# Retrieval products of a two-layer decoder: float32 against three float32r products of split parts

## The chip, the cores and the metric

The kernel runs on one core of one Trainium2 chip. The metric is the device time of one execution in microseconds (us). TensorE is called PE in the rows (its weight loads PEld), VectorE is DVE, ScalarE is ACT, GpSimd is POOL, and SyncE, which issues most of the transfers, is SP.

## The reference

Two decoder layers run over 16 sequences of 128 rows with 256 channels. The change concerns the last sublayer, which this part of the reference describes (its selection of weights is told in words):

```
# x: [16, 128, 256];  gate_w, up_w: [256, 1024];  down_w: [1024, 256]
# down_embed, up_embed: [512, 256]
q        = x @ W_q                        # two halves of 64, scored against two sets of 64 keys
weights  = softmax over the best 8 pairs of keys, spread over the 512 experts
found    = silu(x @ down_embed.T) * weights                       # [.., 512]
out      = (silu(x @ gate_w) * (x @ up_w)) @ down_w + found @ up_embed
x        = layernorm(x + out)
```

All of it is float32. The layers before it are two attentions and a mixture of experts (first layer), and two attentions (second layer).

## The kernel before

The program is a row of stages, each a block in which every engine has its own ordered list of instructions and engines wait on each other by semaphores.

**The second layer** (`second_layer_attentions`, from line 1539) walks through numbered slots. A batch takes a window of 12 slots, and each operation has an offset (the constants before line 1610); each engine goes through the slots and does what falls due. `batch_at(s, offset)` tells which batch is due. SP moves the split parts of queries and keys into stacks by many 64 KB transfers (helper lines 360 to 374), loads rows and context, and in one slot, `SPLIT_KEYS + 3` (line 1669), issues the five loads of the retrieval's weights: gate_w, up_w and down_w of 1 MB each, up_embed and down_embed of 0.5 MB each. POOL splits float32 rows into bf16 parts (helper lines 336 to 342, and lines 2029 and 2033), gathers rows (line 2018) and takes roots (line 2023). ACT does the exponentials (line 1885) and most copies.

**The retrieval** (`retrieve_and_gate`, from line 2214) takes the 16 batches in four turns g of four batches (WIDE is 512 columns), and each turn in eight slabs u of 128 of the 1024 inner channels. The order of PE is written out (before line 2355):

- `gate_and_up(g, u)` (line 2315): two float32 products of 512 columns into the gate bank and two into the up bank. Both banks are double, so it waits until `multiply` is done with slab s-2.
- `find(g, m)` (line 2335), at even u: two products of 512 columns, the rows of one batch against the turned down_embed.
- `down(g, u)` (line 2326), one slab late: four products of 256 columns, the hidden slab against down_w, added into two banks over the whole turn.
- at odd u `turn_weighed` (line 2342, four transposes of the weighed matches), `turn_rows` of the next turn (lines 2301 and 2302, three transposes), `route` (line 2306), and `add_weighed` (line 2349): four products of 256 columns against up_embed into the same banks as `down`.

ACT does Silu of the gate bank (line 2391) and of what was found (2398), the copies out of the transposes' banks (2378, 2403, 2383) and the exponentials (2407), which need another activation table than Silu. DVE multiplies gate and up (`multiply`, line 2520) at the start of every slab; at even u it then picks maxima (`best`), runs `select_weights` and `weigh` (line 2511); at odd u `select_pairs`. At u = 0 it also adds up the rows of the turn before (`add_rows`, 2525), at u = 1 it takes their moments (`spread`, helper lines 464 to 468) and at u = 3 it ends them (`finish`, 2537). POOL has only the 16 roots (line 2442), and three iotas.

Of the kernel before, what the change touches and what calls it, by code (L numbers as in the profile page):

```python
# [8 lines left out]
BF16 = mybir.dt.bfloat16  # L9
I32 = mybir.dt.int32  # L10
# [4 lines left out]
P = 128  # L15
# [1522 lines left out]

def second_layer_attentions(nc, d, t, ps):

    ctx = ExitStack()
    with ctx:
# [27 lines left out]
        ones_row = sb("ones_row_bf", [2, YG * D], BF16)  # L1570

# [8 lines left out]
        ones_made, rows_set = sem("ones_made"), sem("rows_set")  # L1580
        var_m_made, rstd_m_made, var_l_made, rstd_l_made = sem("var_m_made"), sem("rstd_m_made"), sem("var_l_made"), sem("rstd_l_made")
# [28 lines left out]
        STORE_ROWS, TURN_X5, COPY_X5, MAKE_QUERIES, COPY_QUERIES, STORE_QUERIES = 71, 72, 72, 73, 73, 74  # L1610
        query_lane = slots.lane(OWN_SCORES, CROSS_SCORES, SELF1.banks, CROSS1.banks)
# [5 lines left out]
        def _(sp):  # L1617
# [30 lines left out]

            for b in range(2):
                load_rows(b)  # L1650
# [5 lines left out]
            for s in SLOTS:  # L1656
# [10 lines left out]
                if s == SPLIT_KEYS + 3:  # L1667
                    for source, dst in RETRIEVAL_LOADS:
                        sp.dma_start(t[dst][:, :, :], d[source].rearrange("(n p) f -> p n f", p=P)).then_inc(t["retrieval_loaded"], 16)
# [207 lines left out]
        def _(act):  # L1877
# [91 lines left out]

            def copy_queries(b):  # L1970
                if b >= 2:
                    act.wait_ge(queries_stored[b % 2], 16 * (b // 2))
                act.wait_ge(queries_made, b + 1)
                act.activation(queries[b % 2][:, :], small_bank[:, 0:P], ACT.Copy).then_inc(queries_copied, 1)

            for s in SLOTS:
# [31 lines left out]
                if (b := slots.batch_at(s, LAY_X3)) is not None:  # L2008
                    lay_x3(b)

        @block.gpsimd
        def _(pool):
# [33 lines left out]

            gather(0)
            gather(1)
            pool.memset(ones_row[:, :], 1.0).then_inc(ones_made, 1)
            for s in SLOTS:  # L2050
# [16 lines left out]
                if (b := slots.batch_at(s, SPLIT_QUERIES)) is not None:  # L2067
                    split_queries(b)

# [144 lines left out]
def retrieve_and_gate(nc, d, t, ps, out):  # L2214

    ctx = ExitStack()
    with ctx:
# [9 lines left out]
        x5_t = [sb(f"x5_t_{u}", [P, KT + 1, WIDE]) for u in range(2)]  # L2227
# [14 lines left out]
        hidden_t = [sb(f"hidden_t_{u}", [P, WIDE]) for u in range(3)]  # L2242
        found = [sb(f"found_{u}", [P, NEMB]) for u in range(2)]
        weighed = [sb(f"weighed_{u}", [P, NEMB]) for u in range(2)]
        weighed_t = [sb(f"weighed_t_{u}", [P, NEMB // P, P]) for u in range(2)]
# [8 lines left out]
        iotas_made, embed_turned, embed_copied = sem("iotas_made"), sem("embed_turned"), sem("embed_copied")  # L2254
# [9 lines left out]
        loaded, LOADED = t["retrieval_loaded"], t["retrieval_loads"]  # L2264
# [19 lines left out]
        def _(pe):  # L2284
# [19 lines left out]
            def route(g, m):  # L2304
                pe.wait_ge(rows_copied, TOGETHER * g + m + 1)
                pe.matmul(found_bank[:, 3 * P:4 * P], x5_t[g % 2][:, KT, m * P:(m + 1) * P], t["keys"][:, :], start=True, stop=True).then_inc(routed, 1)  # L2306

            def gate_and_up(g, u):
                s = SLABS * g + u
                if s >= 2:  # L2310
                    pe.wait_ge(gated_made, s - 1)
                    pe.wait_ge(hidden_made, s - 1)
                for bank, weights, made in ((gate_bank[s % 2], "gate_w", gate_made), (up_bank[s % 2], "up_w", up_made)):
                    for j in range(KT):
                        mm = pe.matmul(bank[:, :], t[weights][:, j, u * P:(u + 1) * P], x5_t[g % 2][:, j, :], start=(j == 0), stop=(j == KT - 1))  # L2315
                    mm.then_inc(made, 1)

            def down(g, u):
                s = SLABS * g + u
                pe.wait_ge(hidden_made, s + 1)  # L2320
                if u == 0 and g > 0:
                    pe.wait_ge(sum_made, TOGETHER * g)
                if s == 0:
                    pe.wait_ge(embed_copied, KT)
                for m in range(TOGETHER):
                    mm = pe.matmul(acc_bank[m // 2][:, m % 2 * D:(m % 2 + 1) * D], hidden_t[s % 3][:, m * P:(m + 1) * P], t["down_w"][:, u, :],  # L2326
                                   start=(u == 0 and m % 2 == 0), stop=(u == SLABS - 1), skip_group_check=True)
                mm.then_inc(down_made, 1)

            def find(g, m):  # L2330
                b = TOGETHER * g + m
                pe.wait_ge(embed_copied, KT)
                pe.wait_ge(route_copied, routes_before(g, m))
                for j in range(KT):
                    mm = pe.matmul(found_bank[:, :], x5_t[g % 2][:, j, m * P:(m + 1) * P], t["down_embed_t"][:, j, :], start=(j == 0), stop=(j == KT - 1))  # L2335
                mm.then_inc(found_made, 1)

            def turn_weighed(g, m):
                b = TOGETHER * g + m
                pe.wait_ge(weighed_made, b + 1)  # L2340
                for n in range(NEMB // P):
# [3 lines left out]
            def add_weighed(g, m):  # L2345
                b = TOGETHER * g + m
                pe.wait_ge(weighed_copied, b + 1)
# [300 lines left out]
```

## Time and profile before

| | |
|---|---|
| time, median of 3 runs | 1685.72 us (1685.56 to 1687.22) |
| the profiled execution: span from first to last instruction | 1684.2 us |
| PE busy | 1400.9 us (83%) |
| DVE busy | 982.0 us (58%) |
| ACT busy | 609.2 us (36%) |
| POOL busy | 419.8 us (25%) |
| chain that ended last: share by PE | 13% |

The page gives no time of the profiled execution beside its span, so the span is its own time; the median of the runs lies 1.5 us above it. Busy shares are averages over all stages; the last stage, the retrieval, lasts from 1419 us to the end.

### The profile page before, as it was taken

How to read it: one execution, taken by the hardware profiler on the slowest of the kernel's cores; microseconds unless marked ns; L12 is line 12 of the kernel's file. 1: busy time of each engine (PE TensorE's matmuls, PEld its weight loads, DVE VectorE, ACT ScalarE, POOL GpSimd, SP SyncE). 2: the span in 40 equal slices, each digit the busy share in tenths (PEclk: the TensorE clock that was granted, in tenths of full speed). 3: DMA queues.
4: the chain of work that ended last, by engine and by line, in shares of the span. 5: the costliest groups of instructions: out<-in, count | busy, mean ns of one | idle time of the engine just before them, and what ended most of it. 6: DMA issues, size and time to landing. Idle time of an engine off the chain costs nothing. (4 is left out here: it accounts for less than half of the span.)

```text
span 1684.2 us, 29387 instructions
## 1 busy us (share of the span) xinstructions
PE 1400.9 (83%) x9221; PEld 874.6 (52%) x9331; DVE 982.0 (58%) x2623; ACT 609.2 (36%) x1389; POOL 419.8 (25%) x588
## 2 busy tenths in 40 slices
PE   2478999999999954899999946588888875999997
PEld 1245565665665522466566524455555543566654
DVE  5467788787777624222222224577788651676775
ACT  0123444544544421223222223255566542232321
POOL 2242342342341101011111023455555310000000
PEclk9679999999999976999999976799999996999999
DMA  3233443333432106611111123745454311100000
GB/s 91 59 66 60 70 72 52 72 70 55 72 67 37 24 27 226 225 32 38 32 32 33 28 56 109 159 105 114 107 116 111 85 34 50 38 1 13 13 1 26
DMA packets 165337, 112.77 MB, mean 67 GB/s; under 512 B 32690, under 2 KB 155826, under 8 KB 165056
## 3 DMA queue, kind: packets, MB, share of 16 engines
q1 hardware_dynamic: 150272, 99.04, 26.1%
q0 software_dynamic: 3408, 9.31, 2.3%
q10 hardware_dynamic: 11504, 2.53, 0.8%
q8 instruction: 78, 1.28, 0.4%
q14 instruction: 75, 0.61, 0.2%
HBM read 46.48 MB, written 12.45 MB: 35 GB/s over the span
## 5 line engine op out<-in xcount | busy, mean ns | idle before, releaser
L892 ACT ACTIVATE first_probs<-pair 128x512 f32<-128x512 f32 x320 | 189.0, 598 | 231.0 <-PE pair L408 217.4
L449 DVE TENSOR_REDUCE first_negmax_x<-bank 128x2 f32<-128x512 f32 x256 | 177.1, 692 | 59.7 <-PE bank L393 39.8
L393 PE MATMUL bank<-kept_stack_cross 96*128 96x256 bf16 x768 | 151.9, 280 | 11.8 <-DMA kept_stack_cross<-second_parts_x_q 7.5
L1885 ACT ACTIVATE second_probs<-pair 128x512 f32<-128x512 f32 x192 | 113.7, 598 | 130.8 <-PE pair L408 111.6
L408 PE MATMUL pair<-kept_stack_cross 98*128 98x256 bf16 x768 | 148.1, 275 | 3.0 <-ACT first_probs L892 1.0
L1439 PE MATMUL pair<-kept_w,experts_hidden_t 128*128 x312 | 140.5, 593 | 0.0
L449 DVE TENSOR_REDUCE second_negmax_x<-bank 128x2 f32<-128x512 f32 x128 | 88.6, 692 | 59.6 <-PE bank L393 50.5
L393 PEld LDWEIGHTS bank<-kept_stack_cross 96*128 96x128 bf16 x768 | 74.4, 102 | 73.0 <-issue 21.6
L1480 ACT ACTIVATE experts_hidden_t<-bank,kept_b 128x128 f32<-128x128 f32 x156 | 44.6, 368 | 186.4 <-PE bank L1414 186.4
L1394 POOL DMA_INDIRECT experts_expert_rows<-x_mid,kept_row_of x39 | 37.2, 953 | 275.6 <-PE bank L1406 249.1
L386 PE MATMUL bank<-kept_mask_q,kept_ident 128*128 128x512 bf16 x221 | 86.4, 391 | 20.4 <-DVE first_negmax_x L449 11.8
L1439 PEld LDWEIGHTS pair<-kept_w,experts_hidden_t 128*128 128x128 f32 x312 | 59.5, 191 | 74.8 <-issue 74.8
L401 PE MATMUL pair<-kept_mask_t,kept_ident 128*128 128x512 bf16 x249 | 94.7, 380 | 1.8 <-ACT first_probs L892 1.8
L408 PEld LDWEIGHTS pair<-kept_stack_cross 98*128 98x128 bf16 x768 | 74.2, 99 | 41.0 <-issue 2.2
L1517 DVE COPY experts_hidden<-pair 128x512 f32<-128x512 f32 x39 | 27.0, 692 | 107.7 <-PE pair L1439 107.7
L1430 PE MATMUL bank<-kept_w,experts_expert_rows_t 128*128 x156 | 76.8, 617 | 6.3 <-DMA kept_w<-in_L_ffn_W 2.8
L1448 PE MATMUL pair<-kept_w,experts_hidden_t 128*128 x312 | 73.9, 380 | 1.4 <-ACT experts_hidden_t L1488 1.4
L2442 POOL TENSOR_TENSOR retrieve_stats<-retrieve_stats,kept_minus_half 128x1 f32<-128x1 f32 x16 | 8.9, 558 | 251.4 <-DVE retrieve_stats L468 251.4
L438 PE MATMUL pair<-first_probs,kept_v_cross 128*32 128x256 f32 x1024 | 68.5, 385 | 2.8 <-ACT first_probs L892 2.8
L1511 DVE COPY experts_hidden<-bank 128x512 f32<-128x512 f32 x39 | 27.0, 692 | 71.6 <-PE bank L1430 71.6
L1488 ACT ACTIVATE experts_hidden_t<-bank,kept_b 128x128 f32<-128x128 f32 x156 | 44.7, 368 | 50.3 <-PE bank L1422 50.3
L2315 PE MATMUL pair<-retrieve_x_t,kept_gate_w 128*128 128x512 f32 x128 | 61.9, 607 | 0.0
(430 smaller groups left out, 2947.2 us busy)
## 6 DMA issues: line engine op xcount, KB each, us to landing
kept_stack_self<-first_parts_a SPq DMA_DIRECT2D x128, 64.0 KB
kept_w<-in_L_ffn_W SPq DMA_DIRECT2D x16, 512.0 KB, 9.1
kept_w<-in_L_ffn_W SPq DMA_DIRECT2D x8, 1024.0 KB, 9.5
kept_stack_self<-second_parts_a SPq DMA_DIRECT2D x128, 64.0 KB
kept_stack_cross<-first_parts_x_k SPq DMA_DIRECT2D x96, 64.0 KB
kept_stack_cross<-first_parts_x_q SPq DMA_DIRECT2D x96, 64.0 KB
kept_stack_cross<-second_parts_x_k SPq DMA_DIRECT2D x96, 64.0 KB
kept_stack_cross<-second_parts_x_q SPq DMA_DIRECT2D x96, 64.0 KB
```

The costliest lines, as they stand in the source:

```text
L386: pe.matmul(bank[:, :], ident16, mask, start=True, stop=False, skip_group_check=True)
L393: mm = pe.matmul(out, q, k, start=mask is None, stop=True, skip_group_check=True)
L401: pe.matmul(bank[:, :], ident16, mask, start=True, stop=False, skip_group_check=True)
L408: mm = pe.matmul(out, k, q, start=mask is None, stop=True, skip_group_check=True)
L438: mm = pe.matmul(out[j * 32:(j + 1) * 32, at * D:(at + 1) * D], values[:, 2 * k + at, a, j, :], probs[j][:, k * D:(k + 1) * D], start=(a = ...
L449: return dve.tensor_reduce(negmax[:, 2 * n:2 * n + 2], bank[:, :].rearrange("p (m t) -> p m t", t=D), AX.X, ALU.max, negate=True)
L892: act.activation(probs[i % RING][:, :], key_bank[i % 2][:, :], ACT.Exp, scale=att.scale).then_inc(probs_made, 1)
L1430: mm = pe.matmul(layer1_bank[:, :], rows_t[n % 2][:, k, :], t["w1"][:, bass.ds(expert, 1), k, :].rearrange("p a f -> p (a f)"), start=(k = ...
L1439: mm = pe.matmul(layer2_bank[:, :], hidden1_t[n % 2][:, k, :], t["w2"][:, bass.ds(expert, 1), k, :].rearrange("p a f -> p (a f)"), start=( ...
L1448: mm = pe.matmul(layer3_bank[:, 0:D], hidden2_t[n % 2][:, k, :], t["w3"][:, bass.ds(expert, 1), k, :].rearrange("p a f -> p (a f)"), start ...
L1885: act.activation(probs[i % RING][:, :], key_bank[i % 2][:, :], ACT.Exp, scale=att.scale).then_inc(probs_made, 1)
L2315: mm = pe.matmul(bank[:, :], t[weights][:, j, u * P:(u + 1) * P], x5_t[g % 2][:, j, :], start=(j == 0), stop=(j == KT - 1))
```

## The change

Every large float32 product of the retrieval becomes three products of the type float32r. Each operand is kept as a high part (the value written as float32r by ACT) and a low part (the value minus the high part, by POOL, or by DVE for down_embed). `in_parts` multiplies low by high, high by low and high by high. Transposes and `route` stay float32.

```diff
+            def in_parts(to, still, moving, start, stop):
+                (still_high, still_low), (moving_high, moving_low) = still, moving
+                pe.matmul(to, still_low, moving_high, start=start, stop=False, skip_group_check=True)
+                pe.matmul(to, still_high, moving_low, start=False, stop=False, skip_group_check=True)
+                return pe.matmul(to, still_high, moving_high, start=False, stop=stop, skip_group_check=True)
 ...
             def gate_and_up(g, u):
+                if u == 0:
+                    pe.wait_ge(rows_split, TOGETHER * (g + 1))
 ...
-                        mm = pe.matmul(bank[:, :], t[weights][:, j, u * P:(u + 1) * P], x5_t[g % 2][:, j, :], start=(j == 0), stop=(j == KT - 1))
+                        mm = in_parts(bank[:, :], [w[:, j, u * P:(u + 1) * P] for w in t[weights]], [x[:, j, :] for x in x5_t[g % 2]], j == 0, j == KT - 1)
 ...
             def down(g, u):
-                pe.wait_ge(hidden_made, s + 1)
+                pe.wait_ge(hidden_split, s + 1)
```

`down`, `find` and `add_weighed` are changed likewise. `add_weighed` moves from the end of the odd slab to the next even slab, behind `down(g, u - 1)`; that of the turn's last batch stands ahead of the turn's last `down`:

```diff
                 gate_and_up(g, u)
                 if u % 2 == 0:
                     if u == 0 and g > 0:
+                        add_weighed(g - 1, TOGETHER - 1)
                         down(g - 1, SLABS - 1)
                     find(g, u // 2)
                     if u > 0:
                         down(g, u - 1)
+                        add_weighed(g, u // 2 - 1)
                 else:
                     turn_weighed(g, u // 2)
 ...
                     if ahead:
                         route(g + 1, u // 2)
-                    add_weighed(g, u // 2)
+            add_weighed(TURNS - 1, TOGETHER - 1)
             down(TURNS - 1, SLABS - 1)
```

On ACT there are new copies that make the high parts: `rows_first` (128x256) behind each `copy_rows`, `hidden_first` (128x512) behind each `gate`, which waits for `multiply`, and `weighed_first` (128x512) once a batch:

```diff
                 gate(g, u)
+                hidden_first(g, u)
                 if u % 2 == 0:
                     find(g, u // 2)
                 else:
                     copy_weighed(g, u // 2)
                     if ahead:
                         copy_rows(g + 1, u // 2)
+                        rows_first(g + 1, u // 2)
+                    weighed_first(g, u // 2)
+                    if ahead:
                         copy_route(g + 1, u // 2)
```

On POOL the low parts are made, in this order, with the roots between:

```diff
+            for m in range(TOGETHER):
+                rows_rest(0, m)
+            for g, u in units:
+                if g > 0 and u == 2:
+                    roots(g - 1)
+                hidden_rest(g, u)
+                if u % 2:
+                    if g + 1 < TURNS:
+                        rows_rest(g + 1, u // 2)
+                    weighed_rest(g, u // 2)
+            roots(TURNS - 1)
```

DVE gets two subtractions of 128x512 before its first `select_pairs` (the low part of the turned down_embed), and `multiply` waits for `hidden_split` of slab s-2 instead of `down` of slab s-3.

In the second layer only down_embed (0.5 MB) is still loaded at line 1669. The other four tensors come in 14 chunks of 128x512 (256 KB), one in each window of 12 slots: loaded at slot 12c, high part by ACT at slot 12c + 8, low part by POOL at slot 12c + 18:

```diff
+        LOAD_CHUNK, CHUNK_HIGH, CHUNK_LOW = 0, 8, 18
 ...
                 if s == SPLIT_KEYS + 3:
-                    for source, dst in RETRIEVAL_LOADS:
-                        sp.dma_start(t[dst][:, :, :], d[source].rearrange("(n p) f -> p n f", p=P)).then_inc(t["retrieval_loaded"], 16)
+                    sp.dma_start(t["down_embed"][:, :, :], d["L1_ffn_down_embed"].rearrange("(n p) f -> p n f", p=P)).then_inc(t["retrieval_loaded"], 16)
+                if (c := slots.batch_at(s, LOAD_CHUNK)) is not None and c < len(RETRIEVAL_CHUNKS):
+                    load_chunk(c)
 ...
+            def chunk_high(c):
+                act.wait_ge(chunk_loaded[c % 3], 16 * (c // 3 + 1))
+                act.activation(t[dst][0][:, n, f], in_chunk(chunk[c % 3], c), ACT.Copy).then_inc(chunk_high_made, 1)
 ...
+            def chunk_low(c):
+                pool.wait_ge(chunk_high_made, c + 1)
+                pool.tensor_tensor(t[dst][1][:, n, f], in_chunk(chunk[c % 3], c), t[dst][0][:, n, f].bitcast(F32), ALU.subtract).then_inc(chunk_low_made, 1)
```

## Rows read from the trace of the kernel before

**Rows 1.** A stretch: length, busy us of PE PEld DVE ACT POOL, PEclk, DMA

```profile
1490.00:1549.00 59.00, 57.85 (x207) 35.88 (x207) 43.15 (x157) 17.84 (x31) 2.20 (x4) 1.00 0.03 10
```

**Rows 2.** The chain that ended last, shares of the span by line

```profile
PE pair L2315 6%; PE bank L2326 3%; PE bank L2349 2%; PE bank L2335 1%; PE bank L2342 0%; PE bank L2306 0%; PE bank L2301 0%; DVE retrieve_sum_o L2525 0%; DVE retrieve_weighed L2511 0%; DVE retrieve_wt L2491 0%; DVE retrieve_wt L2498 0%; DVE retrieve_wt L2494 0%; PE bank L2302 0%; ACT retrieve_x_t L2378 0%; DMA retrieve_q<-queries 0%
```

**Rows 3.** Timeline of PE: first turning, an odd slab, the last products

```profile
1443.23 0.66 PE L2342 MATMUL bank<-kept_ident,retrieve_weighed 128*128 128x128 f32 x4 [0.43 <-DVE retrieve_weighed L2511]
...
1456.32 1.88 PE L2315 MATMUL pair<-retrieve_x_t,kept_up_w 128*128 128x512 f32 x4
1458.04 0.60 PE L2342 MATMUL bank<-kept_ident,retrieve_weighed 128*128 128x128 f32 x4
...
1458.80 1.89 PE L2326 MATMUL bank<-kept_down_w,retrieve_hidden_t 128*128 128x256 f32 x8
...
1671.47 1.89 PE L2326 MATMUL bank<-kept_down_w,retrieve_hidden_t 128*128 128x256 f32 x8
```

**Rows 4.** Timeline of PE in the second layer, bf16 products

```profile
1159.10 0.38 PE L386 MATMUL bank<-kept_causal_q,kept_ident 128*128 128x512 bf16 x1
1159.31 0.39 PE L393 MATMUL bank<-kept_stack_self 96*128 96x128 bf16 x4
```

**Rows 5.** Timeline of DVE, slabs 0 to 3 of the second turn

```profile
1497.35 1.42 DVE L2525 TENSOR_TENSOR retrieve_sum_o<-bank,retrieve_x 128x256 f32<-128x256 f32 x4 [0.29 <-PE bank L2326]
...
1503.57 0.69 DVE L2520 TENSOR_TENSOR retrieve_hidden_t<-retrieve_gated,pair 128x512 f32<-128x512 f32 x1
...
1512.12 0.69 DVE L2520 TENSOR_TENSOR retrieve_hidden_t<-retrieve_gated,pair 128x512 f32<-128x512 f32 x1
...
1517.50 0.75 DVE L2511 SCALAR_TENSOR_TENSOR retrieve_weighed<-retrieve_found,retrieve_rz,retrieve_wt 128x512 f32<-128x512 f32 x1
...
1518.73 0.69 DVE L2520 TENSOR_TENSOR retrieve_hidden_t<-retrieve_gated,pair 128x512 f32<-128x512 f32 x1 [0.47 <-PE pair L2315]
...
1523.28 1.38 DVE L2537 TENSOR_SCALAR retrieve_result<-retrieve_sum_o,retrieve_stats 128x256 f32<-128x256 f32 x4
```

**Rows 6.** Timeline of ACT, from the table change to the next Silu

```profile
1499.74 1.28 ACT L2407 ACT_TABLE_LOAD   x1
...
1502.88 0.60 ACT L2391 ACTIVATE retrieve_gated<-pair 128x512 f32<-128x512 f32 x1
```

**Rows 7.** Two lines: count, duration ns least/median/most, first and last start

```profile
L2029 POOL TENSOR_TENSOR second_rest_a<-second_full_a,second_parts_a x16: 1158/1167/1172, 1004.5 to 1308.9; 128x512 f32<-128x512 f32 x16
...
L2099 DVE SCALAR_TENSOR_TENSOR second_sum_m<-second_routed,kept_shares,second_sum_m x16: 483/736/759, 991.5 to 1285.3; 128x256 f32<-128x256 f32 x16
```

**Rows 8.** Timelines of SP and PE around the five loads

```profile
1045.88 0.59 SPq L1669 DMA_DIRECT2D kept_gate_w<-in_L_ffn_gate_w  x1
...
1068.33 0.61 PE L393 MATMUL bank<-kept_stack_cross 96*128 96x256 bf16 x2 [7.47 <-DMA kept_stack_cross<-second_parts_x_q]
```

**Rows 9.** Timeline of POOL: the first gather of four batches, one root

```profile
1052.95 1.05 POOL L2018 DMA_INDIRECT second_routed<-expert_out,kept_slots  x1 [0.17 <-issue]
...
1080.04 1.05 POOL L2018 DMA_INDIRECT second_routed<-expert_out,kept_slots  x1 [0.17 <-issue]
...
1122.35 1.05 POOL L2018 DMA_INDIRECT second_routed<-expert_out,kept_slots  x1 [0.17 <-issue]
...
1133.65 0.57 POOL L2023 TENSOR_TENSOR second_stats_l<-second_stats_l,kept_minus_half 128x1 f32<-128x1 f32 x1 [2.50 <-DVE second_stats_l L468]
...
1143.08 1.05 POOL L2018 DMA_INDIRECT second_routed<-expert_out,kept_slots  x1 [0.17 <-issue]
```

**Rows 10.** Timeline of ACT, where the change puts a chunk's high part

```profile
1154.80 0.60 ACT L1885 ACTIVATE second_probs<-pair 128x512 f32<-128x512 f32 x1 [2.19 <-PE pair L408]
```

**Rows 11.** Timeline of PE: a pause and the slow product behind it

```profile
1360.35 0.41 PE L1821 MATMUL pair<-kept_ident,second_x 128*128 128x128 f32 x2 [2.03 <-DVE second_x L2160]
...
1361.24 1.22 PE L1827 MATMUL pair<-kept_wq_ret,second_x_t 128*128 128x128 f32 x4 [0.25 <-ACT second_x_t L1968]
...
1376.42 0.71 PE L1827 MATMUL pair<-kept_wq_ret,second_x_t 128*128 128x128 f32 x4 [0.25 <-ACT second_x_t L1968]
```

More of the change, by code:

```diff
@@ L9 @@
 BF16 = mybir.dt.bfloat16
+F32R = mybir.dt.float32r
 I32 = mybir.dt.int32
@@ L1536, in _, with chunks_of, in_chunk @@
                     finish(n - 2)
+CHUNK = 512
+def chunks_of(source, dst, rows, width):
+    step = min(width, CHUNK)
+    tall = CHUNK // step
+    return [(source, dst, slice(n, n + tall), slice(f, f + step)) for n in range(0, rows // P, tall) for f in range(0, width, step)]
+RETRIEVAL_CHUNKS = (chunks_of("L1_ffn_gate_w", "gate_w", D, INTER) + chunks_of("L1_ffn_up_w", "up_w", D, INTER) +
+                    chunks_of("L1_ffn_down_w", "down_w", INTER, D) + chunks_of("L1_ffn_up_embed", "up_embed", NEMB, D))
+def in_chunk(tile, c):
+    _, _, n, f = RETRIEVAL_CHUNKS[c]
+    return tile[:, :].rearrange("p (n f) -> p n f", n=n.stop - n.start)
 def second_layer_attentions(nc, d, t, ps):
@@ L1570, in second_layer_attentions @@
         ones_row = sb("ones_row_bf", [2, YG * D], BF16)
+        chunk = [sb(f"chunk_{u}", [P, CHUNK]) for u in range(3)]
         bank_a, work, out_x, small_bank = ps[0], ps[1], ps[4], ps[5]
@@ L1580, in second_layer_attentions @@
         ones_made, rows_set = sem("ones_made"), sem("rows_set")
+        chunk_loaded, chunk_high_made, chunk_low_made = [sem(f"chunk_loaded_{u}") for u in range(3)], sem("chunk_high_made"), sem("chunk_low_made")
         var_m_made, rstd_m_made, var_l_made, rstd_l_made = sem("var_m_made"), sem("rstd_m_made"), sem("var_l_made"), sem("rstd_l_made")
@@ L2009, in _ @@
                     lay_x3(b)
+                if (c := slots.batch_at(s, CHUNK_HIGH)) is not None and c < len(RETRIEVAL_CHUNKS):
+                    chunk_high(c)
+            act.wait_ge(chunk_high_made, len(RETRIEVAL_CHUNKS))
         @block.gpsimd
@@ L2068, in _ @@
                     split_queries(b)
+                if (c := slots.batch_at(s, CHUNK_LOW)) is not None and c < len(RETRIEVAL_CHUNKS):
+                    chunk_low(c)
+            pool.wait_ge(chunk_low_made, len(RETRIEVAL_CHUNKS))
         @block.vector
@@ L2226, in retrieve_and_gate @@
         q01 = [sb(f"q01_{b}", [P, 2, NKEY]) for b in range(B)]
-        x5_t = [sb(f"x5_t_{u}", [P, KT + 1, WIDE]) for u in range(2)]
+        full_t = [sb(f"full_t_{u}", [P, KT + 1, P]) for u in range(2)]
+        x5_t = [[sb(f"x5_t_{part}_{u}", [P, KT, WIDE], F32R) for part in ("high", "low")] for u in range(2)]
+        down_embed_t = [sb(f"down_embed_t_{part}", [P, KT, NEMB], F32R) for part in ("high", "low")]
         routing = [sb(f"routing_{m}", [P, 2, NKEY + TOPK]) for m in range(TOGETHER)]
@@ L2410, in _ @@
                 copy_rows(0, m)
+                rows_first(0, m)
                 copy_route(0, m)
@@ L2540, in _ @@
                 best(0, m)
+            for j in range(KT):
+                dve.wait_ge(embed_copied, j + 1)
+                dve.tensor_tensor(down_embed_t[1][:, j, :], acc_bank[j][:, :], down_embed_t[0][:, j, :].bitcast(F32), ALU.subtract).then_inc(embed_split, 1)
             dve.wait_ge(iotas_made, 3)
```

111 lines of the change are left out of this document (78 added, 33 removed).

## The prediction, made before the changed kernel was run

> **What bounds the kernel now.** I read the stretches first, then the chain, then timelines engine by engine. In a typical stretch of the retrieval PE is busy 57.85 of 59 us at full clock, DVE 43.15, ACT 17.84, POOL 2.20 [rows 1]; the chain that ended last is nearly all PE, and its four costliest lines are those that the change rewrites [rows 2]. So a shorter PE shortens this stage, until the next engine binds. The second layer is another regime: its engines hand work to each other, and in one place transfers land late.
>
> **PE's part.** A float32 product is two records. Four records of 512 columns take 1.72 us to the next instruction (1456.32 to 1458.04), so a product takes 0.86, and one of 256 columns half of that, 0.43 [rows 3]. At 2.4 GHz that is four cycles a column. Gate and up have 128 products (110 us), find 32 (27.5), down 128 (55), add_weighed 64 (27.5): 220 us. No row shows a float32r product, so I bound one: below by bf16, 512 columns in 0.21 us, one cycle a column [rows 4]; above by a float32 record, which takes two cycles a column whatever it does, the transposes too: seven of 128 columns in 0.76 us, 1458.04 to 1458.80 [rows 3]. Three products are then 3 or 6 cycles where 4 stood: 165 us (55 less) or 330 (110 more). I take one cycle: float32's four look like four passes over the parts of two operands, of one cycle each, and a product of parts needs one. The Trainium skill (FP8 and Floating Point Precision, section TensorE Precision Notes) says that true FP32 is four passes and that the reduced kind reads 4 bytes and truncates them; the trace agrees on the four and shows nothing of the other.
>
> **What is late next.** A pair of slabs needs, on PE, three quarters of 220/16 and 1.0 for transposes and route: 11.3 us, now 14.75. But it is also a loop through DVE. From the end of `weigh`: turned weights and rows 0.76, down 12 x 0.107 = 1.3, route 0.2 with 0.15 of waiting for ACT's copies, gate and up 12 x 0.2145 = 2.6, a start of 0.3: 5.3 to 5.4 until the next even `multiply`. From that to the end of its weigh 1517.50 + 0.75 - 1512.12 = 6.1 [rows 5]. Together 11.5: PE and DVE are nearly level, and what DVE has beyond the pair stops PE. It has more: slab 1 lasts from 1503.57 to 1512.12, 8.55, where slab 3 with `finish` takes 1518.73 to 1524.66, 5.9, of which finish is 1.4; so multiply with select_pairs is 4.5 and spread 4.0; add_rows is 1.4 [rows 5]. ACT gets 2.2 us of copies a pair by its usual lengths, beside 17.84 busy in 59; they hide, except at slab 6. From the exponentials' table load to the next Silu are 3.1 us [rows 6]; the load now begins some 4.1 after weigh (behind two high parts and the route's copy), so that multiply comes at 7.2 and not at 5.4: 1.8 in each turn with a successor.
>
> Turn by turn:
> - First. It starts 0.7 later (the last rows_first and rows_rest come before the first product) and DVE has two more subtractions (1.4), less some slow PE time that goes. The first turning of weights comes at 1443.7, now at 1443.2 [rows 3]. Then three pairs of 11.5, 1.8 for slab 6, and 5.1 to the end of the next gate and up: 1485.2.
> - Second and third, from that end: multiply and best to 1.65, the wait for the moved add_weighed and the last down to 2.9, add_rows to 4.3, weigh to 9.1; select_pairs and spread to 17.65 (PE is ready at 14.5); weigh 23.8; slab 3 to 29.7; weigh 35.8; multiply 43.0; weigh 49.1; end 54.2. So 54.2 a turn, twice: 1593.6.
> - Last. The same without route, best and next rows: 45.2 at the last gate and up. Then the last weights: ACT's copies to 48.0, POOL's subtraction of 1.17 [rows 7] behind the hidden slab's, to 49.3, add_weighed and down 2.6: 51.9, at 1645.5. Now PE ends at 1671.47 + 1.73 = 1673.2 [rows 3].
>
> Gain 27.7 us, half of what PE drops. What follows the last product (add_rows, spread, finish, the stores) stays.
>
> **What takes from it.** (a) POOL works 4.2 us a pair where it was idle (three times 1.17, once 0.67). A DVE instruction with two operands in SBUF takes 483 ns at its fastest and 736 at the median, in batches where POOL works beside it [rows 7]. Six of 512 columns in each pair have that form. Where select_pairs meets POOL, the pair has 1 us to spare; where select_weights does, not: I take 0.2 a pair and 0.5 in each spread slab, 4.2. Bounds: nothing, and 34 (the third rival). (b) PE now pauses 2.7 us before the first turning of a later turn. Behind a pause of 2.03 a line took 1.22 us that takes 0.71 elsewhere [rows 11], as at 1.2 GHz in place of 2.4. Such a dip lies largely inside DVE's spread; I count 3 for all, between 0 and 10. The retrieval then gives 27.7 - 4.2 - 3 = 20.5.
>
> **The second layer.** The loads of 4 MB begin at 1045.88; behind them PE waits 7.47 us for a stack of queries, until 1068.33 [rows 8]. Neighbouring gathers are 27.1 us apart there and 20.7 at 1122.35 [rows 9]. Now 0.5 MB stays in that place. Gain 6.4 by that pitch; bounds 0 (the batches behind catch up) and 12; I take 7, for the slow clock behind it. Against it stand 14 chunks. ACT's 0.6 us of a high part falls into an idle 2.19 [rows 10]. POOL's 1.17 falls before a root that waits 2.50 for DVE [rows 9]; without that cover the latent rows would come 1 us later in each batch, 14 in all. SP issues one more transfer ahead of the stack of queries, the next rows and the first self parts, by the rows 0.59 [rows 8]; the stacks are used slots later. I take 0.07 a batch, 1 us; bounds 0 and 8. Net gain 6.
>
> **Sum.** 1684.2 - 20.5 - 6 = 1657.7, and 1.5 for the median's distance from the profiled span: 1659.
>
> **The rivals.**
> - PE stays the bound. For it: its share of the chain today [rows 2]. Against: DVE's sum above. Then all 55 come, and 6: 1684.2 - 61 + 1.5 = 1625.
> - A float32r product takes two cycles a column, slower than before: one mechanism, in each of 1056 products. For it: every float32 record of the trace goes at that pace [rows 3]. Against: what float32 does in its four cycles. 1684.2 + 110 - 6 + 1.5 = 1790. The loss starts at some 1.35 cycles a column, where three products cost PE what one float32 product did and the second layer's 6.
> - POOL and DVE exclude each other. The mechanism: POOL's 4.2 us of each pair cannot run while DVE is in a form with two SBUF operands, half of its time, and each meeting is paid in full: 2.1 in 16 pairs, 34 in place of 4.2: 1689. For it: the 736 ns [rows 7]. Against it: part of the meetings falls into `select_pairs`, where DVE has time to spare, and that instruction lost 253 ns and not all of the overlap. The Trainium skill (GPSIMD Engine Reference, section 8, Key points) warns of contention with just these forms, without a price; the trace agrees that there is some.
> - The burst was slack, and the chunks cost 2: the retrieval's 20.5 without the 6: 1667.
> - The change does not do what it says (float32r passes as full float32, twelve cycles): 440 more, 1 in 100, counted with the second.
>
> **The numbers.** Forecast 0.63, PE-bound 0.10, two cycles 0.10, exclusion 0.05, slack burst 0.12. The forecast's own range is 1644 to 1674 (dips, contention and the second layer at their bounds, not all at once). The range of 8 in 10 takes in the slack burst and part of PE-bound: 1630 to 1680. A measurement can tell 0.2%, 3.4 us: faster 0.86 (forecast, PE-bound, burst, a little of the exclusion), same 0.03, slower 0.11.
>
> **What would show it.** Float32r records of 512 columns 0.21 us apart (right) or 0.43 (second rival). PE busy 55 us less in the retrieval, DVE over 75%, and the weights' transposes waiting for `weigh`; if they do not wait, PE is still the bound. Turns of 54 us. Slab 6's multiply late behind ACT's table load. Forms with two SBUF operands clearly over 0.69 us would show the contention. In the second layer no wait of 7 us near 1060 and later gathers still 20.7 apart; wrong if these grow by over 0.5.

## The result, and the profile after

| | before | after |
|---|---|---|
| median of 20 runs each | 1685.86 us (1682.01 to 1697.22) | 1699.78 us (1685.13 to 1711.32) |
| profiled execution, its span | 1684.2 us | 1698.3 us |
| retrieval, from the first transpose of down_embed | 1419.2, lasts 265.0 us | 1425.2, lasts 273.1 us |

The ratio is 1.0054 (95%: 1.0035 to 1.0072): slower by about 9 us, where 1659 us was forecast. The medians lie 13.9 us apart; three executions of the changed kernel, of 1710.7 to 1711.3 us, were in a slower state, and the ratio leaves them out. In the profiled executions both stages went the wrong way: the second layer ends 6.0 us later, and the retrieval takes 8.1 us more, where the forecast had 20.5 less.

The whole retrieval, before and then after (stretch, length, busy us of PE PEld DVE ACT POOL, PEclk, DMA):

```profile
1419.20:1684.20 265.00, 246.17 (x856) 152.35 (x856) 178.01 (x656) 70.91 (x127) 9.28 (x19) 0.96 0.07 21
```

```profile
1425.20:1698.30 273.10, 218.45 (x1208) 188.94 (x1208) 221.25 (x658) 102.82 (x191) 87.67 (x83) 0.90 0.07 20
```

PE is 28 us less busy, half of the 55 that the prediction named. Its granted clock fell from 0.96 to 0.90 (from 1445 to 1670 us it was 1.00 before and is 0.94 after), and its products are a little slower than I took (below). DVE is 43.2 us busier with two instructions more, which take 1.3 us. The stretch of [rows 1], after, and the chain that ended last by engine:

```profile
1490.00:1549.00 59.00, 48.01 (x272) 41.89 (x272) 51.81 (x152) 24.88 (x46) 20.45 (x19) 0.94 0.03 10
```

```profile
DVE 7%; DVEq 4%; PE 3%; issue 1%; ACT 1%; POOL 0%; DMA 0%; SPq 0%; ACTq 0%
```

The chain of [rows 2] was PE's; now it is DVE's. PE's own rows answer to [rows 3]: float32r products of 512 columns start 0.227 us apart at full clock (21 steps from 1441.81 to 1446.57), about one cycle a column, 6% more than the 0.2145 that I took. Those of 256 columns start 0.118 us apart (five steps from 1529.93 to 1530.52), where I took 0.107.

```profile
1441.81 0.39 PE L2368 MATMUL pair<-retrieve_x_t_high,kept_up_w_high 128*128 128x512 f32 x1
1442.04 0.39 PE L2366 MATMUL pair<-retrieve_x_t_high,kept_up_w_low 128*128 128x512 f32 x1
```

And what PE waits for in the retrieval (us in total, times, longest):

```profile
PE bank L2407 <- DVE retrieve_weighed L2635: 35.0, 16, 5.7
```

Which instructions of DVE grew? The tile `rank_hot` before, then `rank_hot` and `part` after (count, ns least/median/most, first and last start):

```profile
L2469 DVE TENSOR_TENSOR retrieve_rank_hot<-retrieve_iota,retrieve_at x16: 680/681/683, 1434.3 to 1655.5; 128x512 f32<-128x512 f32 x16
```

```profile
L2593 DVE TENSOR_TENSOR retrieve_rank_hot<-retrieve_iota,retrieve_at x16: 681/1456/1473, 1441.8 to 1668.2; 128x512 f32<-128x512 f32 x16
L2596 DVE TENSOR_TENSOR retrieve_rank_hot<-retrieve_rank_hot,retrieve_falling x16: 679/1792/1797, 1442.7 to 1670.8; 128x512 f32<-128x512 f32 x16
L2610 DVE TENSOR_TENSOR retrieve_part<-retrieve_picked,retrieve_raised x16: 215/1062/1112, 1445.6 to 1673.8; 128x64 f32<-128x64 f32 x16
```

The grown ones read two operands from SBUF. The reduction of 512 columns (`rank`), which reads one, keeps its 676 ns, and `multiply`, which reads one of its two from PSUM, keeps 685; but in this run neither ever meets a subtraction of POOL, so that their lengths here decide nothing (e1 below has such a meeting). The timeline of the grown ones beside POOL's says how (start, us):

```profile
1510.26 1.28 POOL L2548 TENSOR_TENSOR retrieve_hidden_t_low<-retrieve_hidden,retrieve_hidden_t_high 128x512 fp32r<-128x512 f32 x1 [7.54 <-ACT retrieve_hidden_t_high L2472]
1511.57 1.10 POOL L2542 TENSOR_TENSOR retrieve_x_t_low<-retrieve_full_t,retrieve_x_t_high 128x256 fp32r<-128x256 f32 x1
1512.64 1.29 POOL L2554 TENSOR_TENSOR retrieve_weighed_t_low<-retrieve_turned_w,retrieve_weighed_t_high 128x512 fp32r<-128x512 f32 x1
```

```profile
1510.63 1.45 DVE L2593 TENSOR_TENSOR retrieve_rank_hot<-retrieve_iota,retrieve_at 128x512 f32<-128x512 f32 x1
1512.16 0.60 DVE L2595 TENSOR_TENSOR retrieve_picked<-retrieve_left,retrieve_sums 128x64 f32<-128x64 f32 x1
1512.68 1.79 DVE L2596 TENSOR_TENSOR retrieve_rank_hot<-retrieve_rank_hot,retrieve_falling 128x512 f32<-128x512 f32 x1
```

POOL's first subtraction ends at 1511.54; the comparison ends at 1512.08, 0.54 later, having done nothing before some 1511.4 (it takes 0.68). POOL's next one takes 1.10 us instead of 0.72, since DVE holds until 1512.08. `picked` (0.225 us alone) ends 0.09 after it, at 1512.76. The product of 512 columns starts within 0.04 us of POOL's third and ends 0.54 after it. So the two take turns, each for a whole instruction. The Trainium skill says just this (SBUF — State Buffer, section Who interferes with whom): whoever starts first has the shared pair of ports for the whole instruction and the other fully blocks, and a DVE instruction with two SBUF inputs contends with a GpSimd one that reads SBUF; the trace agrees, by these rows.

### The profile page after: what moved, and what is told of

Read it like the earlier page. It is cut to its first block and busy times, and to the rows that moved or that the text cites. A ratio compares the mean times of both kernels' runs of the same rounds, so it can differ in the third digit from the quotient of the medians.

```text
span 1698.3 us, 30333 instructions
## 1 busy us (share of the span) xinstructions
PE 1385.9 (82%) x9573; PEld 915.9 (54%) x9683; DVE 1027.9 (61%) x2625; ACT 648.9 (38%) x1467; POOL 515.4 (30%) x666
## 5 line engine op out<-in xcount | busy, mean ns | idle before, releaser
L1395 POOL DMA_INDIRECT experts_expert_rows<-x_mid,kept_row_of x39 | 37.2, 953 | 275.9 <-PE bank L1407 249.7
L387 PE MATMUL bank<-kept_mask_q,kept_ident 128*128 128x512 bf16 x221 | 86.5, 391 | 20.3 <-DVE first_negmax_x L450 11.9
L2548 POOL TENSOR_TENSOR retrieve_hidden_t_low<-retrieve_hidden,retrieve_hidden_t_high 128x512 fp32r<-128x512 f32 x32 | 41.3, 1290 | 148.3 <-ACT retrieve_hidden_t_high L2472 148.3
L1012 POOL TENSOR_TENSOR first_stats_a<-first_stats_a,kept_minus_half 128x1 f32<-128x1 f32 x16 | 8.8, 551 | 211.8 <-DVE first_stats_a L469 211.8
```

The costliest lines, as they stand in the source:

```text
L387: pe.matmul(bank[:, :], ident16, mask, start=True, stop=False, skip_group_check=True)
```

## The experiments

All ratios are to the kernel before, with the 95% interval in brackets; starts and lengths of the retrieval are from the profiles.

| kernel | ratio | retrieval starts, lasts, us |
|---|---|---|
| changed kernel | 1.0054 [1.0035, 1.0072] | 1425.2, 273.1 |
| e1 low parts narrow | 0.9932 [0.9910, 0.9954] | 1426.0, 249.7 |
| e5 narrow, and scratch | 1.0027 [0.9999, 1.0054] | 1421.8, 266.0 |
| e4 float32, POOL beside it | 1.0107 [1.0082, 1.0132] | 1420.8, 285.3 |
| e14 low parts on DVE | 1.0110 [1.0084, 1.0137] | 1430.3, 278.1 |
| e6 turned later | 1.0096 [1.0065, 1.0127] | 1411.7, 285.0 |
| e9 rows before hidden | 1.0007 [0.9985, 1.0029] | 1416.2, 266.3 |
| e13 first down later | 1.0001 [0.9981, 1.0021] | 1414.8, 269.3 |
| e3 down float32 | 0.9954 [0.9934, 0.9974] | 1419.5, 258.8 |
| e8 the same, turned later | 0.9808 [0.9763, 0.9852] | 1417.5, 234.1 |
| e10 the same, loads in slot 7 | 0.9805 [0.9787, 0.9824] | 1416.2, 234.0 |

The lengths of the retrieval repeat from profile to profile: the five kernels with the float32 retrieval have 265.0 (before), 264.5 (e2), 264.7 (e7), 264.5 (e12) and 264.7 us (e15), the changed kernel and e11, which has the same retrieval, 273.1 and 272.8. Its starts do not repeat: the second layer is the same program in the changed kernel, e1, e5, e6, e9 and e14, and it ends between 1411.7 and 1430.3 us. So one profile settles what a change of the retrieval is worth there, and what the second layer costs is read from the ratios.

### Does POOL hold DVE, and what is it worth?

**e1.** The changed kernel with narrow low parts:

```diff
-                pool.tensor_tensor(low[:, :], hidden[s % 2][:, :], high[:, :].bitcast(F32), ALU.subtract).then_inc(hidden_split, 1)
+                few = WIDE if s < 3 else 8
+                pool.tensor_tensor(low[:, 0:few], hidden[s % 2][:, 0:few], high[:, 0:few].bitcast(F32), ALU.subtract).then_inc(hidden_split, 1)
```

and `rows_rest`, `weighed_rest` likewise.

> The changed kernel, but from the third turn on (rows), from slab 3 on (hidden) and from batch 2 on (weighed) POOL makes only 8 columns of each low part (the others keep the values of their buffer's first use), so POOL's work in the retrieval falls from 88 us to some 20. Exclusion theory (a DVE instruction with two SBUF operands waits for the whole of a POOL subtraction): the comparison and the product of 512 columns go back from 1456 and 1792 ns to about 685, `part` from 1110 to 220, DVE's busy time from 221 to about 182, and the retrieval shortens from 273 by 25 to 30 us: 1672 in all (1666 to 1680). Rival A (the loss comes from PE pausing and the slower clock behind pauses): DVE's forms may shorten but the retrieval stays above 265: over 1690. Rival B (second layer took it all): the retrieval was fine, under 4 us change.

As the exclusion theory had it: 249.7 us, 23.4 less (I had said 25 to 30), DVE is 182.6 us busy, and the forms are back.

```profile
L2596 DVE TENSOR_TENSOR retrieve_rank_hot<-retrieve_iota,retrieve_at x16: 680/681/1403, 1442.3 to 1649.5; 128x512 f32<-128x512 f32 x16
```

In e1's first turn, where some subtractions are still full, the reduction meets two of them, one from 1467.68 to 1468.93 us and the one shown, and keeps its length. The 64-column comparison behind it, which has two operands in SBUF and takes 0.22 us alone, ends with the second:

```profile
1468.54 0.68 DVE L2603 TENSOR_REDUCE retrieve_rank<-retrieve_rank_hot 128x64 f32<-128x512 f32 x1
1468.89 1.30 POOL L2557 TENSOR_TENSOR retrieve_weighed_t_low<-retrieve_turned_w,retrieve_weighed_t_high 128x512 fp32r<-128x512 f32 x1
1469.13 1.14 DVE L2604 TENSOR_TENSOR retrieve_one_hot<-retrieve_iota,retrieve_at 128x64 f32<-128x64 f32 x1
```

`multiply` stands in a meeting once in e8 (1572.44 us, beside a subtraction of 1.24 us that began at 1571.88) and takes 0.68 us there too.

**e5.** e1 shortens POOL's part of each chain too. Here e1 gets full-width scratch work behind each narrow subtraction:

```diff
+            def subtract(columns):
+                pool.drain()
+                pool.tensor_tensor(idle[2][:, 0:columns], idle[0][:, 0:columns], idle[1][:, 0:columns], ALU.subtract)
```

> The kernel with narrow low parts (8 columns, from the third turn's rows, slab 3 and batch 2 on), and behind each narrow subtraction a full-width one between scratch tiles, which nobody waits for. PE and DVE get their low parts as early as with the narrow ones, but POOL is busy as in the changed kernel. Exclusion: the time goes back to the changed kernel's, 1697 (1690 to 1703), comparison and product of 512 columns over 1200 ns. Rival (the narrow kernel was faster because PE and multiply got the low parts sooner): stays at 1677 (1672 to 1681).

Between the two: 266.0, 16.3 of the 23.4 us, though POOL is busier here (106.1 us) than in the changed kernel (87.7). The form I named kept its 682 ns; others were met instead, `picked` above all (64 columns, 1146 ns at the median, 226 at the least), and DVE's busy time went from 182.6 to 211.3. The other 7 us may be the earlier low parts or other meetings; the run doesn't part them.

**e4.** The kernel before, with that `subtract` of 512 columns behind each `multiply`, and 256 and 512 behind a pair's copies.

> The kernel before with all its float32 products, and on POOL the same subtractions as in the changed kernel (512 columns a slab, 256 and 512 a pair, about 4 us a pair), but between scratch tiles that nobody reads. Exclusion theory: DVE's forms with two SBUF operands stretch here too (512 columns to 1400 to 1800 ns where a subtraction runs, `part` to about 1100 ns), DVE's busy time in the retrieval goes from 178 to 205 to 220, while the time grows little, because a pair has 14.75 us on PE against 11.5 + 2.6 on DVE: 1686 to 1694. Rival (the stretching belongs to float32r outputs or to waiting inside the changed kernel's order): forms stay at 680 to 690 ns, DVE at 178, time 1686.

The stretching needs no float32r: DVE 226.1 us busy instead of 178.0. Even a conversion of 16 columns, with one operand, is stretched, from 175 ns to 745 at the median.

But I missed the time: the retrieval is 20.3 us longer. Nobody waits here for what POOL makes, so this is the price of the meetings alone, in the order of before; PE's waits for `weigh` went from 3.9 to 19.1 us. I took 14.75 less 11.5 for the slack of a pair, and 11.5 was the forecast's loop of shorter products. By the rows of before the loop is 14 us: 6.1 from multiply to the end of weigh, then turning, down, route, add_weighed, gate and up (some 7.9). There is less than 1 us to spare in 14.75.

**e14.** The changed kernel with `rows_rest`, `hidden_rest` and `weighed_rest` issued by DVE:

```diff
                 if u % 2 == 0:
+                    hidden_rest(g, u)
                     select_weights(g, u // 2)
                     weigh(g, u // 2)
...
+                else:
...
+                    hidden_rest(g, u)
+                    if ahead:
+                        rows_rest(g + 1, u // 2)
+                    weighed_rest(g, u // 2)
```

> The changed kernel, but DVE makes the low parts of the retrieval itself (hidden 32 x 0.69, weighed 16 x 0.69, rows 16 x 0.37 us: 39 us more of DVE), in even slabs behind best, in odd ones behind select_pairs; POOL has only the roots. Exclusion theory: POOL's subtractions took 39 us from DVE by stretching its forms, as much as DVE needs to do them, so giving the work back costs about nothing: DVE busy 218 to 222 us, no stretched form, time 1697 (1690 to 1704). Rival (POOL's part was mostly in parallel after all): 1712 or more, by some 1 us a pair.

1708.15 us, outside my 1690 to 1704. DVE's busy time, 214.4 against the changed kernel's 221.3, is even below my 218 to 222, and no form is stretched, but the retrieval is 5.0 longer than the changed kernel's. So POOL's 78 us of work saved 5 us of retrieval in the profiles, and 0.56%, 9 us, by the ratios, which take in how much the second layer scatters.

### Is it the loop, or DVE itself?

**e3.** Gate, up and find in parts; `down` and `add_weighed` as before, their weights loaded straight; POOL has only `rows_rest`:

```diff
-                    mm = in_parts(acc_bank[m // 2][:, m % 2 * D:(m % 2 + 1) * D], [h[:, m * P:(m + 1) * P] for h in hidden_t[s % 3]],
...
+                    mm = pe.matmul(acc_bank[m // 2][:, m % 2 * D:(m % 2 + 1) * D], hidden_t[s % 3][:, m * P:(m + 1) * P], t["down_w"][:, u, :],
...
```

> Only gate, up and find are three float32r products; down and add_weighed stay single float32 products, with their weights loaded straight in six of the 14 chunks, so that POOL has only the rows' low parts (0.67 us a pair of slabs) and eight chunks in the second layer. PE drops by 128 x (0.86 - 3 x 0.227) + 32 x (0.86 - 3 x 0.227) = 29 us. Exclusion theory: nearly all of it arrives (POOL 0.67 instead of 4.2 us a pair, contention at most 8 us in all), retrieval 237 to 245 us, time 1655 (1648 to 1665). Rival A (pauses, clock): DVE's loop has as many links as in the changed kernel, the retrieval stays near 265, time 1680 to 1690.

The exclusion theory alone was wrong here: 258.8 us, not 237 to 245, though all forms of 512 columns have their lengths of before (only `picked`, of 64 columns, is stretched, to 591 ns). The second turn took 60.5 us from its first multiply to the next turn's, where 60.4 stood before: PE's shorter products gave nothing there. PE waits for `weigh`, and what it does behind that wait comes slowly:

```profile
1516.66 1.11 PE L2408 MATMUL bank<-kept_ident,retrieve_weighed 128*128 128x128 f32 x4 [2.12 <-DVE retrieve_weighed L2603]
...
1518.20 2.83 PE L2393 MATMUL bank<-kept_down_w,retrieve_hidden_t 128*128 128x256 f32 x8
```

Eight records that take 1.89 us in [rows 3] take 2.83 behind a pause of 2.12, at a granted clock of 0.66 on average. In this order down, add_weighed, gate and up all lie between `weigh` and the next `multiply`.

**e6 and e8.** Both turn the weights behind the next slab's gate and up, so that PE has work while DVE weighs; `add_rows` moves behind the turn's first `weigh`. e6 keeps all products in parts (and adds the weighed matches in the odd slab, since their low parts come later); e8 is e3 in that order:

```diff
                 gate_and_up(g, u)
+                before = (g, u // 2 - 1) if u else (g - 1, TOGETHER - 1)
                 if u % 2 == 0:
+                    if before[0] >= 0:
+                        turn_weighed(*before)
                     find(g, u // 2)
                     if u > 0:
                         down(g, u - 1)
+                    if before[0] >= 0:
+                        add_weighed(*before)
...
                 else:
-                    turn_weighed(g, u // 2)
```

> The changed kernel with all its products and low parts, in another order: the weighed matches are turned behind the next slab's gate and up, their products come a slab later still, and the sums over a turn are added behind the first weigh of the next. PE no longer has to wait for weigh before it may do the next gate and up, so the loop multiply, select_weights, weigh, turning, gate and up (6.1 + 5.4 us and the stretches by POOL) is open. If that loop is what passes the exclusion on to the time: DVE alone binds, 221 us busy and some 20 of starts and ends, retrieval 240 to 248, time 1672 (1666 to 1680). If the exclusion loads DVE itself and the loop does not matter: under 8 us faster than the changed kernel, 1690 to 1700.

> Gate, up and find as three float32r products, down and add_weighed in float32, and the order in which the weighed matches are turned behind the next gate and up. POOL has only the rows' low parts, DVE is busy 180 to 190 us, PE 218 us at full clock. Loop theory (that kernel in the old order was held by the loop weigh, turning, down, add_weighed, gate and up, multiply, weigh: 15.4 us a pair): now PE's own work binds, 12.95 us a pair and 10 of ends, retrieval 225 to 235, time 1650 (1644 to 1658). Rival (PE's clock or the exclusion held it): 1675 to 1681 as in the old order.

e8 is faster by 1.9%, as the loop theory had it: pairs of 13.07 us, DVE 180.8 us busy, no wait of PE for `weigh`, and a granted clock of 1.00 from 1433 to 1640 us. e3 had 17.4 us of such waits, and low clock behind some of them, of the 24.7 us between the two; e8 has neither, so the runs don't part the waits from the clock. e6 got nothing (its retrieval is 11.9 us longer than the changed kernel's), and its own row says why: ACT's copy of the next rows stood behind the hidden slab's high part, which waits for `multiply`.

```profile
1520.04 0.79 PE L2361 MATMUL bank<-kept_keys,retrieve_full_t 128*128 128x128 f32 x2 [4.34 <-ACT retrieve_full_t L2453]
```

**e9.** That queueing taken away:

```diff
+                copy_rows(g + 1, u // 2)
+                rows_first(g + 1, u // 2)
+                copy_route(g + 1, u // 2)
                 hidden_first(g, u)
-                    copy_rows(g + 1, u // 2)
...
```

> All products in three parts, the late turning of the weights as before, but ACT copies the next rows and the route (and does find's Silu) ahead of the hidden slab's high part, which waits for multiply. In the kernel before this one route waited up to 4.3 us for a copy of rows that stood behind that high part, twice a turn or more, and the retrieval lasted 285 us. If that queueing is what ate the order's gain: PE's waits for full_t vanish, DVE binds with its 221 us and some 20 of ends, retrieval 240 to 250, time 1675 (1668 to 1684). If POOL's subtractions hold DVE in any order and the loop was never the matter: 1692 or more.

18.7 us from the retrieval, but not 40. Within the second turn the pairs are 12.1, 12.5 and 14.2 us; at its start one takes 21.8, with PE waiting for `add_rows`:

```profile
1498.72 0.55 PE L2366 MATMUL bank<-kept_down_w_high,retrieve_hidden_t_low 128*128 128x256 f32 x1 [4.46 <-DVE retrieve_sum_o L2658]
```

**e13.** The turn's first `down` moves from slab 1 to slab 2, behind the next `find`; chunk loads in slot 7.

> All products in parts, late turning, rows before the hidden slab's high part, chunk loads in slot 7; new: in slab 1 PE does route without waiting, and the first down of a turn, which needs add_rows, moves to slab 2. In the kernel before this one three pairs of a turn took 12.1, 12.4 and 14.2 us, and the one at the turn's start 21.8, with PE waiting 4.5 us for add_rows and route behind it. Theory: with DVE 221 us busy the pair at the start falls to 18 or 19 us; retrieval 254 to 260; with the spread loads intact 1672 (1668 to 1678), ratio 0.991. Rival: the stretched forms hold DVE there as well (it never idled in that pair): no more than 3 us from the retrieval, ratio 0.996 or more.

The rival was right: 269.3 us, no gain. The pair at the start fell to 19 us and the others rose to 14 and 15. DVE is 220 to 224 us busy in e6, e9 and e13. Four orders of the same work gave 285.0, 273.1, 269.3 and 266.3 us, none the 240 to 250 that I expected of two of them. That every order stays above DVE's 221 us is shown; that no better one exists is not.

### The second layer

**e2, e7, e12, e15.** All have the retrieval of before. e2 and e15 load the 14 chunks straight into float32 tiles; e7 and e12 take them through the three buffers, with ACT's and POOL's work. e2 and e7 load in slot 0, e12 and e15 in slot 7:

```diff
-        LOAD_CHUNK, CHUNK_HIGH, CHUNK_LOW = 0, 8, 18
+        LOAD_CHUNK, CHUNK_HIGH, CHUNK_LOW = 7, 20, 30
```

**e11** is the changed kernel with this line alone; **e10** is e8 with it.

> The kernel before with float32 products, but four of its five weight loads come as 14 transfers of 256 KB, one in each window of 12 slots, straight into their tiles; no high or low parts. If the burst cost what I forecast (6 to 7 us that stay): 1679.5 (1678 to 1681) against 1685.9. Rival (what is gained near 1060 us is lost again behind, because the batches catch up or the transfers disturb others): 1685 to 1687, with gathers 7 us earlier at 1100 and level again by 1300.

> The retrieval of the kernel before (float32 products, no low parts), and the second layer of the changed kernel: 14 chunks through three buffers, a copy by ACT into the float32 tile and a subtraction by POOL whose result nobody reads. With transfers straight into the tiles the same spread was 5 us faster than before. If ACT's and POOL's work on the chunks gives that back (root of the latent rows behind POOL's 1.27 us, my bound of 14 us): 1686 to 1692. If that work hides, as forecast: 1682 (1680 to 1684).

> Retrieval of the kernel before, second layer of the changed kernel with its chunks split, loads in slot 7. Collision theory: the full gain of the spread loads arrives, 6 to 8 us: ratio 0.9955, 1679. Rival (splitting costs it): ratio 0.999 to 1.001 as with slot 0.

> The kernel before with its weight loads as 14 transfers straight into the tiles, in slot 7 of the window instead of slot 0. With slot 0: ratio 0.9970. Collision theory (chunk and the 8 KB of sums issued together): the 23 to 25 us batches go here too, 2 to 4 us faster than with slot 0, ratio 0.995, 1678. Rival (only the splitting of chunks suffered in slot 0): ratio 0.997 again.

> The changed kernel with nothing altered but the slot of the chunks' loads (7 in place of 0, parts at 20 and 30 in place of 8 and 18). Collision theory (chunk and sums are issued within 0.2 us of each other, and the sums land late): no wait of DVE for the sums, gathers 20.5 us apart, retrieval starts at 1412 to 1416 instead of 1425: 1692 (1688 to 1695). Rival (the splitting by ACT and POOL costs it): as the changed kernel, 1697 to 1700.

> Gate, up and find in parts, down and add_weighed float32, late turning, and each chunk's load moved from slot 0 to slot 7 of the window (high and low part at 20 and 30), away from the 8 KB transfer of the sums. Collision theory: the batches of 23 to 25 us, in which DVE waits 1 to 3 us for the sums, disappear; 2 to 5 us faster than the same kernel with slot 0 (0.981 of before): ratio 0.978 to 0.980, 1652. Rival (those batches come from elsewhere): ratio 0.981 or worse.

| | loads in slot 0 | in slot 7 |
|---|---|---|
| straight into the tiles | e2 0.9970 [0.9954, 0.9986] | e15 0.9946 [0.9926, 0.9965] |
| split by ACT and POOL | e7 1.0010 [0.9984, 1.0036] | e12 0.9973 [0.9956, 0.9990] |
| the changed kernel | 1.0054 [1.0035, 1.0072] | e11 1.0019 [0.9998, 1.0040] |

The spread loads alone gave 5 us in slot 0, where I expected 6 to 7 (e2), and 9 in slot 7 (e15, as expected). In each row slot 7 is faster, by 0.24, 0.37 and 0.35% (4 to 6 us); the two intervals of a row overlap, so it is the three rows together that speak for it. Between e8 and e10, where I expected 0.1 to 0.3%, no difference shows, and e8's interval of 0.9% could hide one. In slot 0 SP issues the chunk at the moment at which ACT issues the 8 KB of sums on which DVE's reciprocals wait (changed kernel, SP and ACT, then DVE):

```profile
1220.42 0.59 SPq L1678 DMA_DIRECT2D second_chunk<-in_L_ffn_down_w  x1
1220.46 0.61 ACTq L1992 DMA_DIRECT2D second_sums<-second_heads_x  x1
```

```profile
1226.61 0.25 DVE L2190 RECIPROCAL second_recips<-second_sums 128x16 f32<-128x16 f32 x1 [3.01 <-DMA second_sums<-second_heads_x]
```

This batch lasts 25.15 us from gather to gather, where 20.5 is usual. In the profiles with slot 0 the long batches (23 us and more from gather to gather, behind 1130 us) are those with such a wait, 0.7 to 3.0 us; e7 has five, e2 three, e6 none. With slot 7 there is none in e15 and e11 and one in e10, e12 and e13. The kernel before, which has no chunks at all, has one as well (23.1 us from 1164, with a wait of 0.8). So the 8 KB can come late without a chunk beside them; that the 256 KB delay them is my reading of this coincidence, and not shown. The splitting costs 0.40% in slot 0 and 0.27% in slot 7, 7 and 5 us, so that e12 fell between its two expectations, while e7 and e11 came as the first of theirs said; no row that I read names the place of this cost.

The version to keep is e10: 1655.33 us median, 0.9805. In the stretch that answers to [rows 1], from 1485 to 1544 us, PE no longer stops: it is busy for all 59.00 us, DVE for 50.60, POOL for 5.42.

## Why the prediction was wrong, step by step

- **PE's rate: right in kind.** About one cycle a column; the second rival (two) is out, and "it doesn't do what it says" too. Over all products 0.227 and 0.118 us in place of 0.2145 and 0.107 are some 12 us of PE's time, an estimate from these rows, and the lower clock is most of the rest: PE dropped 28 us and not 55.
- **What is late next: right in kind.** DVE and its loop bind, PE waits for `weigh` 16 times, and PE-bound is out. In size it was short: e1, with 28 us of POOL's 78, has turns of 56.5 and 58.0 us where 54.2 stood, and a retrieval of 249.7 where the forecast without contention gives 244.5 - 4.2 = 240.3. So 9.4 us of the miss were in this sum, by e1's price of (a). Counted from the end of its first gate and up, e1's second turn has the multiplies of slabs 2, 4 and 6 at 17.9, 29.8 and 43.9 us and ends at 56.5, where I had 17.65, 29.7, 43.0 and 54.2: the steps hold up to slab 4 and are short behind it. PE's pace is a part, 24 products of the loop in each pair, 0.28 us, or some 4.5 us in 16 pairs (an estimate from the rows above); DVE's forms in e1 are still 3.3 us longer than before (182.6 less 178.0 and 1.3); and PE paused 11 times for 20.4 us in all at a mean clock of 0.94, so term (b), 3 us for dips, is a part. No run parts the three.
- **(a), contention at 4.2 us: wrong, and the largest term.** POOL's subtractions took 42 us of DVE's time. Of the retrieval they took 23.4 us by e1, 16.3 by e5, and 20.3 in the order of before by e4. So the step that failed is the price of a meeting of POOL and DVE. The third rival had the mechanism right and the price too high (34); I gave it 0.05. The row that I rested on, 736 ns at the median against 483, showed the exclusion already: at each of its 11 long ones DVE starts 0.2 to 0.3 us behind a POOL subtraction of 0.67 to 0.75 us and ends 0.28 behind it; the five that meet no such subtraction take 483 to 486 ns. One of them (start, us):

```profile
1076.52 0.67 POOL L342 TENSOR_TENSOR second_parts_x_q<-second_rest_x_q,second_parts_x_q 128x256 bf16<-128x256 f32 x1 [0.16 <-issue]
1076.71 0.76 DVE L2099 SCALAR_TENSOR_TENSOR second_sum_m<-second_routed,kept_shares,second_sum_m 128x256 f32<-128x256 f32 x1
```

I read its 253 ns as the price of any meeting. The price is what is left of POOL's instruction, up to 1.1 us, and for a 64-column instruction of 0.22 us that makes five times its length. I had counted only the forms of 512 columns; `part` and `picked`, of 64, took 15 of the 42 us. "In select_pairs the pair has 1 us to spare" failed with it: there three subtractions meet three such instructions, some 2.3 us a pair.
- **The miss in the retrieval** is 273.1 - 244.5 = 28.6: 23.4 - 4.2 = 19.2 for (a), and the 9.4; with e5's price of (a) it would be 12.1 and 16.5.
- **The second layer, 6 us of gain: right alone, lost together.** Without the burst the kernel gains 9 us (e15), more than my 7. PE's wait of 7.47 [rows 8] is gone and the gathers of [rows 9] are 19.4 apart in place of 27.1. I gave the chunks 1 us. The slot costs 4 to 6 and the splitting 5 to 7: e7, which is this part alone, is 2 us slower than before, with an interval that includes none. Of the new transfer I looked at SP's queue and at the stacks behind it, and not at what else is due at the same moment. What exactly the slot and the splitting delay stays open.
- **The sum:** 8.1 us longer in the retrieval, 2 in the second layer by e7 (with an interval that includes none): 10, and 9 were measured. The 6 us by which the profiled execution's second layer ended later are within its scatter.

## What to carry to other kernels

Before you give an idle POOL work, list what DVE runs at that moment with two operands in SBUF, the short instructions too: in this kernel each meeting cost DVE about the rest of POOL's instruction, so 78 us of "free" POOL work saved 5 to 9 us against DVE doing it. A shorter product pays only where PE doesn't wait for another engine in the same loop: the same products gave 0.5% in the old order and 1.9% with the weights turned one slab later. When a bulk load is cut into pieces, try more than one moment for them: here the slot alone was worth 4 to 6 us. Where a row's median lies far above its least, as 736 over 483 ns did here, put the timelines of both engines side by side before you set a price.

## What was not expected of the hardware

- The exclusion also stops POOL: a subtraction of 256 columns takes 1.10 us instead of 0.72 behind a DVE instruction.
- Some one-operand forms are stretched too where POOL works: the conversion of 16 columns from 0.175 to 0.745 us at the median in e4. The reduction of 512 columns is not (e1, 0.68 us beside two subtractions).
- POOL's subtraction of 512 columns took 1.26 to 1.30 us with float32r and with float32 results alike (changed kernel, e7), where [rows 7] has the 1.17 that I had taken. That row subtracts a bf16 part (`parts_a`), the new ones a second operand of 4 bytes; in e7 both kinds stand side by side, at 1.17 and 1.27.
